# A second set of buffers for the front of a pair, the residual added on TensorE, and small products split into two row halves

## What is computed

```
block 0   attention in 8x8 windows, 4 heads of 12 channels, with a bias table; x = x + proj(attn)
          g = a * sigmoid(b), (a, b) = w1 x;  x = x + leaky(conv3x3(pad_edge(g)))
block 1   x  = x + dwconv3x3_cpe1(x)
          y  = layernorm over channels (x);  act = silu(W_act y);  y = W_in y
          t  = silu(dwconv3x3(y));  q, k = elu(W_qk t) + 1;  v = t
          z  = 1 / (q . mean(k));  kv = rope(k)^T v per head;  attn = (rope(q) kv) z + dwconv3x3_lepe(v)
          x  = x + W_out(attn * act)
          x  = x + dwconv3x3_cpe2(x)
          x  = x + W_fc2 gelu(W_fc1 layernorm(x))
```

## Time and profile before

| | |
|---|---|
| median of 3 runs | 790.66 us (789.95 to 791.23) |
| the profiled execution | 786.9 us |
| its span on the core | 784.9 us |
| PE busy | 671.9 us (86%), mean granted clock 0.898 |
| DVE busy | 528.8 us (67%) |
| ACT, POOL busy | 423.4 us, 312.9 us |

### The profile page before, as it was taken

One profiled execution on the slowest core, in us unless ns is written; L12 is line 12 of the kernel. 1 busy time (PEld: TensorE's weight loads), 2 busy tenths in 40 slices (PEclk: granted clock), 3 DMA queues, 4 the chain that ended last, 5 costly groups with the idle time before them and its releaser, 6 DMA issues. The chain is left out here.

```text
span 784.9 us, 21749 instructions
## 1 busy us (share of the span) xinstructions
PE 671.9 (86%) x9580; PEld 385.9 (49%) x9580; DVE 528.8 (67%) x575; ACT 423.4 (54%) x517; POOL 312.9 (40%) x200
## 2 busy tenths in 40 slices
PE   5899989879899999876888999888987994686795
PEld 3576545547545555445644455465433442562242
DVE  6668307999989434599889333899992128998702
ACT  3578237958464386585342587685304755513334
POOL 8433301547655211115965120138870000677300
PEclk9999999979989999897979999977899996555799
DMA  4200122000001022100000122000000110000001
GB/s 101 56 21 18 44 67 63 18 2 18 4 15 32 18 63 56 38 17 2 18 1 2 32 63 63 17 2 2 2 1 15 50 50 26 1 3 0 1 2 46
DMA packets 19471, 20.55 MB, mean 26 GB/s; under 512 B 8784, under 2 KB 18128, under 8 KB 19378
## 3 DMA queue, kind: packets, MB, share of 16 engines
q1 hardware_dynamic: 17810, 18.95, 8.9%
q10 hardware_dynamic: 1568, 0.22, 0.2%
HBM read 8.39 MB, written 3.54 MB: 15 GB/s over the span
## 5 line engine op out<-in xcount | busy, mean ns | idle before, releaser
L1400 POOL TENSOR_TENSOR SC<-SC,mx 128x768 f32<-128x768 f32 x48 | 81.8, 1705 | 218.5 <-DVE mx L1200 218.5
L1258 DVE SCALAR_TENSOR_TENSOR CT<-TP,vec_sb,CT 112x768 f32<-112x768 f32 x96 | 148.5, 1566 | 0.8
L658 PE MATMUL ps<-ZP,wdw 48*64 48x384 f32 x1728 | 145.9, 488 | 3.4 <-DMA ZP<-YF 2.4
L1244 DVE SCALAR_TENSOR_TENSOR QS<-ZP,vec_sb,QS 112x768 f32<-112x768 f32 x96 | 111.9, 1200 | 0.6
L658 PEld LDWEIGHTS ps<-ZP,wdw 48*64 48x64 f32 x1728 | 73.3, 134 | 73.5 <-issue 34.2
L1196 DVE TENSOR_TENSOR SC<-ps,bias_sb 128x768 f32<-128x768 f32 x48 | 45.7, 952 | 63.0 <-PE ps L723 35.5
L658 PE MATMUL ps<-G,w_sb 48*64 48x384 f32 x864 | 75.1, 499 | 1.7 <-DVE X1T L1213 1.4
L1230 DVE TENSOR_TENSOR LV<-LV,XB 112x768 f32<-112x768 f32 x24 | 25.5, 1064 | 73.1 <-ACT LV L1048 73.1
L942 ACT ACT_TABLE_LOAD x52 | 66.7, 1283 | 0.9
L1371 POOL TENSOR_TENSOR KC<-KK,rope_th_sb 98x384 f32<-98x384 f32 x12 | 18.0, 1496 | 106.2 <-DVE KK L1264 106.1
L658 PEld LDWEIGHTS ps<-G,w_sb 48*64 48x64 f32 x864 | 36.4, 138 | 39.1 <-issue 30.6
(11 more groups left out here) (166 smaller groups left out, 1239.4 us busy)
## 6 DMA issues: line engine op xcount, KB each, us to landing
ZP<-YF SPq DMA_DIRECT2D x48, 75.0 KB, 2.2
XR<-in_x_dram SPq DMA_DIRECT2D x24, 144.0 KB, 2.8
X1T<-in_x_dram SPq DMA_DIRECT2D x24, 144.0 KB, 2.8
XA<-XB SPq DMA_DIRECT2D x48, 72.0 KB, 2.2
out_dram<-XB SPq DMA_DIRECT2D x24, 144.0 KB, 2.3
rope_th_sb<-in_rope_th_dram SPq DMA_DIRECT2D x1, 441.0 KB
w_sb<-in_w_dram SPq DMA_DIRECT2D x2, 81.0 KB, 2.6
wfc_sb<-in_wfc_dram SPq DMA_DIRECT2D x4, 36.0 KB
```

The lines of the kernel that those rows point to most:

```text
L658: mm = pe.matmul(slot(job)[half(c, HALF), r * BANK:r * BANK + SPX], w[half(r), tap * HALF:(tap + 1) * HALF], shifted(t, d * CROWS + c * WI ...
L1244: dve.scalar_tensor_tensor(out=rows16(T0[n]), in0=win, scalar=wt, in1=rows16(T0[n]), op0=ALU.mult, op1=ALU.add).then_inc(dwc_step, 1)
L1258: dve.scalar_tensor_tensor(out=ct, in0=win, scalar=wt, in1=ct, op0=ALU.mult, op1=ALU.add).then_inc(lepe_step, 1)
L1400: pool.tensor_tensor(sc, sc, bc_last(mx[:, (q % NSC) * 12:(q % NSC) * 12 + 12], TOK), ALU.subtract).then_inc(sub_ready, 1)
```

## The change

What it does:
- ZP is kept for block 0's result and d0 alone. A second padded image ZI takes what ie and oz write, and c1 and d3 read it. py of pair i+1 waits for d0 of pair i in place of d3; ie of pair i+1 waits for d3 of pair i.
- x3 writes XF, a state buffer of its own, freed by op; xc and yn read it. The layer norm of the front works in two buffers LF, that of the back and z in the two chunks left of LV.
- XA and pa are gone. op now multiplies in two column halves and adds the state by products of XF with an identity (eye2) into the same PSUM sums: 4 + 4 matmuls in place of 2. oz adds only a bias.
- tr, kt and vt are done in two row halves: 12, 16 and 16 products in place of 6, 8 and 8, each with half the contraction rows and half the columns streamed; the halves write different PSUM banks, and pt, ke, ko, kr, ve and kv read the new layout.
- For space: PT has 5 buffers in place of 6, KC and KS one in place of two (so kr waits for the kv before), kv_turn shares km_sb.
- All five order strings are new.

Of the order strings only the stretch around the last front stands here; the rest of the diff is cut to what carries it.

```diff
@@ PE_ORDER
-    q.2.0@3 av.3.2@0 kv.2.0@2 kt.2.1@1 pj.3.2@0 q.2.1@2 w1a.3.1@1 kt.2.2@0 q.2.2@3 vt.2.1@1 vt.2.2@0 kv.2.1@1
-    w1b.3.2@1 kv.2.2@0 kp.2.0@0 w1a.3.2@2 dn.2.2@0 dn.2.0@3 cv.3.0@1 at.2.0@3 dn.2.1@2 cv.3.1@1 at.2.1@0 op.2.0@1
-    cv.3.2@2 op.2.1@0 at.2.2@1 d3.2.0@0 xc2.2.0@0 va2.2.0@0 op.2.2@1 f11.2.0@0 d3.2.1@1 f10.2.0@0 xc2.2.1@1 f12.2.0@3
-    va2.2.1@1 d3.2.2@0 f2.2.0@3 xc2.2.2@0 f10.2.1@1 f12.2.1@2 va2.2.2@0 f11.2.1@3 d0.3.0@1 f2.2.1@0 f11.2.2@2
-    f10.2.2@3 xc.3.0@1 d0.3.1@0 f12.2.2@3 va.3.0@2 xc.3.1@0 f2.2.2@3 va.3.1@0 d0.3.2@1 ip.3.0@0 ip.3.1@2 ac.3.0@3
+    cv.3.1@0 kv.2.2@2 q.2.1@3 kp.2.0@2 q.2.2@0 dn.2.0@2 cv.3.2@1 dn.2.1@3 at.2.0@2 dn.2.2@0 d0.3.0@1 op.2.0@2 at.2.1@3
+    xc.3.0@2 d0.3.1@1 op.2.1@3 d0.3.2@2 xc.3.1@1 at.2.2@0 d3.2.0@1 op.2.2@0 va.3.1@1 va.3.0@3 d3.2.1@0 ip.3.0@1
+    ip.3.1@3 d3.2.2@2 xc2.2.1@1 ac.3.0@0 xc2.2.0@3 xc.3.2@1 va2.2.0@3 va.3.2@1 va2.2.1@3 f11.2.0@1 ip.3.2@3 f10.2.0@0
...
@@ DVE_ORDER
+    az.2.1 am.2.1 c20.2.2 c21.2.2 c22.2.2 c23.2.2 c24.2.2 c25.2.2 c26.2.2 c27.2.2 oz.2.1 az.2.2 c28.2.2 am.2.2 oz.2.2
+    yn.3.0 yn.3.1 c10.3.0 c11.3.0 c12.3.0 c13.3.0 c14.3.0 yn2.2.0 c15.3.0 yn.3.2 c16.3.0 yn2.2.1 c17.3.0 c10.3.1
...
@@ SP: py
-                        wait_filled(sp, last(*[("d3", i - 1, d) for _, d in near(i, n)]))
+                        wait_filled(sp, last(*[("d0", i - 1, d) for _, d in near(i, n)]))
...
-                elif name == "pa":
-                    wait_read(sp, ("d0", i, n))
-                    if i:
-                        wait_read(sp, ("op", i - 1, n))
...
@@ PE: tr, kt, op
-                    for j in range(6):
-                        mm = pe.transpose(slot(job)[:, j * 128:(j + 1) * 128], SC[q % NSC][:, j * 128:(j + 1) * 128],
-                                          ident_sb[:, :])
+                        for r in range(2):
+                            at = r * BANK + j * HALF
+                            mm = pe.transpose(slot(job)[:, at:at + HALF],
+                                              SC[q % NSC][half(r, HALF), j * 128:(j + 1) * 128],
+                                              ident_sb[half(r, HALF), half(r, HALF)])
...
-                        mm = pe.matmul(slot(job)[0:TT, j * 128:j * 128 + R],
-                                       two_rows(1 + n * CROWS + 2 * j, K1), wlk_sb[:, :], start=True, stop=True)
+                        for r in range(2):
+                            rows = slice(r * HALF, r * HALF + C + 1)
+                            mm = pe.matmul(slot(job)[0:TT, r * BANK + j * C:r * BANK + (j + 1) * C],
+                                           two_rows(1 + n * CROWS + 2 * j, rows), wlk_sb[rows, 0:C],
+                                           start=True, stop=True)
...
-                    product(job, wq("out"), CT[(i * CH + n) % 2])
+                    wait_slot(pe, job)
+                    image = [half(c, HALF if c == 0 else C) for c in range(2)]
+                    for b in range(2):
+                        for c in range(2):
+                            pe.matmul(slot(job)[image[c], b * BANK:b * BANK + SPX], wq("out")[:, image[c]],
+                                      CT[(i * CH + n) % 2][:, b * SPX:(b + 1) * SPX], start=True, stop=False)
+                    for r in range(2):
+                        for c in range(2):
+                            at = n * CPX + c * SPX
+                            mm = pe.matmul(slot(job)[image[c], r * BANK:r * BANK + SPX],
+                                           eye2_sb[half(r), 0:HALF if c == 0 else C],
+                                           XF[half(r), at:at + SPX], start=False, stop=True)
...
@@ ACT: x3, ie
-                        act.wait_ge(stored[n], 32 * i)
-                    act.activation(pairs(chunk(XB, n)), two(job), ACT.Identity, bias=v("cpe1_b"))\
+                        wait_filled(act, ("op", i - 1, n))
+                    act.activation(pairs(chunk(XF, n)), two(job), ACT.Identity, bias=v("cpe1_b"))\
...
-                    wait_filled(act, ("d0", i, halo_last(n)))
-                    act.activation(inner8(ZP, n), two8(job), ACT.Identity, bias=inp_b2).then_inc(free(job), 2)
+                    if i:
+                        wait_filled(act, last(*[("d3", i - 1, d) for _, d in near(i, n)]))
...
+                    act.activation(inner8(ZI, n), two8(job), ACT.Identity, bias=inp_b2).then_inc(free(job), 2)
...
@@ DVE: oz
-                    dve.wait_ge(xa_placed[n], 64 * (i + 1))
-                    dve.scalar_tensor_tensor(out=inner8(ZP, n), in0=two8(job), scalar=v("out_b"),
-                                             in1=chunk(XA, n).rearrange("p (b y x) -> p b y x", b=2, x=W),
-                                             op0=ALU.add, op1=ALU.add).then_inc(free(job), 2)
+                    dve.tensor_scalar(inner8(ZI, n), two8(job), v("out_b"), None, ALU.add).then_inc(free(job), 2)
...
@@ POOL: kr
+                old = before(i, n, 1)
+                if old:
+                    wait_filled(pool, ("kv",) + old)
```

More of the change, by code:

```diff
@@ L46 @@
 SQ = ["q", "k", "v", "w1a", "w1b", "act", "inp", "lq", "lk", "out"]
-KEPT = ["act", "inp", "out"]
+KEPT = ["out"]
 TURN = ["q", "k", "w1a", "w1b"]
@@ L894, in run @@
                     pe.wait_ge(yn2_ready, YN2_COUNT["yn2", i, n])
-                    turned(job, wfc1_sb[:, m * HALF:(m + 1) * HALF], chunk(LV, n))
+                    turned(job, wfc1_sb[:, m * HALF:(m + 1) * HALF], nbuf(n))
                 elif name == "f2":
@@ L1041, in run @@
                     wait_filled(act, job)
-                    act.activation(pairs(chunk(LV, n)), two(job), ACT.Square).then_inc(free(job), 2)
+                    old = before(i, n, NFR)
+                    if name == "sq" and old:
+                        wait_filled(act, last(("ip",) + old, ("ac",) + old))
+                    if name == "sq2" and n >= NFR:
+                        wait_filled(act, last(*[(f"f1{m}", i, n - NFR) for m in range(FG)]))
+                    dst = LF[kc % NFR] if name == "sq" else nbuf(n)
+                    act.activation(pairs(dst), two(job), ACT.Square).then_inc(free(job), 2)
                 elif name in ("rs", "rs2"):
@@ L1045, in run @@
                     wait_filled(act, job)
-                    act.activation(pairs(chunk(LV, n)), two(job), ACT.Ln, bias=eps_ln).then_inc(free(job), 2)
+                    dst = LF[kc % NFR] if name == "rs" else nbuf(n)
+                    act.activation(pairs(dst), two(job), ACT.Ln, bias=eps_ln).then_inc(free(job), 2)
                     wait_read(act, job)
-                    act.activation(chunk(LV, n), chunk(LV, n), ACT.Exp, scale=-0.5)\
+                    act.activation(dst, dst, ACT.Exp, scale=-0.5)\
                        .then_inc(rstd_ready if name == "rs" else rstd2_ready, 1)
@@ L1070, in run @@
                     wait_filled(act, job)
-                    act.activation(KK[n % 2].rearrange("p (t c) -> p t c", c=R),
-                                   slot(job)[0:TT, :].rearrange("p (t c) -> p t c", c=128)[:, :, 0:R],
-                                   ACT.Exp, bias=minus1[0:TT, :]).then_inc(free(job), 1)
+                    act.activation(pairs(KK[n % 2]), two(job, TT), ACT.Exp, bias=minus1[0:TT, :])                       .then_inc(free(job), 1)
                 elif name == "qe":
@@ L1085, in run @@
                         wait_filled(act, ("kv",) + old)
-                    act.activation(VT.rearrange("p (t b c) -> p t b c", b=2, c=C),
-                                   slot(job)[0:TT, :].rearrange("p (t b c) -> p t b c", b=2, c=HALF)[:, :, :, 0:C],
-                                   ACT.Copy).then_inc(free(job), 2)
+                    act.activation(pairs(VT), two(job, TT), ACT.Copy).then_inc(free(job), 2)
                 elif name == "z":
@@ L1091, in run @@
                     wait_filled(act, job)
-                    act.activation(pairs(chunk(LV, n)), two(job), ACT.Ln, bias=eps_z).then_inc(free(job), 2)
+                    if n >= NFR:
+                        act.wait_ge(am_ready, AM_COUNT["am", i, n - NFR])
+                    act.activation(pairs(zbuf(n)), two(job), ACT.Ln, bias=eps_z).then_inc(free(job), 2)
                     wait_read(act, job)
-                    act.activation(chunk(LV, n), chunk(LV, n), ACT.Exp, scale=-1.0).then_inc(z_ready, 1)
+                    act.activation(zbuf(n), zbuf(n), ACT.Exp, scale=-1.0).then_inc(z_ready, 1)
                 elif name[:2] == "ge":
@@ L1314, in run @@
                     wait_filled(dve, job)
-                    dve.tensor_tensor(pairs(chunk(LV, n)), two(job), pairs(chunk(LV, n)), ALU.mult).then_inc(free(job), 2)
+                    dve.tensor_tensor(pairs(zbuf(n)), two(job), pairs(zbuf(n)), ALU.mult).then_inc(free(job), 2)
                 elif name == "am":
```

306 lines of the change are left out of this document (154 added, 152 removed).

## The result

The changed kernel takes 715.59 us (median of 4 runs, 712.72 to 719.18) beside 790.83 us (4 runs) for the kernel before: a ratio of 0.906, 95% interval 0.9025 to 0.9091, 75 us less. The profiled execution took 712.72 us, its span is 710.9 us. Ratios are taken from fast runs alone, and only e6 has slower ones: 723.28 and 722.01 of its four, which leaves 711.05 and 719.76.

What follows compares the result with a forecast made beforehand. PE and DVE waiting for each other in turn was taken as the bound. Start 125.3 + W 454 + last gap 2 + end 141.7 = 723.0, + 5.8 to the median = 728.8 us; range 700 to 770.

Steps and rivals of the forecast that it cites:

- W: Stretch from pair 0's first tap to pair 2's last d3: 489.2 us before, 454 forecast with PE at 88%.
- The last gap: Between pair 2's last d3 and pair 3's first tap: 2 us in place of 34.9, which gives 32.9.
- The other two gaps: From last d3 of pairs 0 and 1 to the next first tap, 47.4 and 36.8 us: merge with the tap stretches.
- W's work: PE's full-rate work in W: 417.0 after moves, +4 for op, -21.5 for the halves, in sum 399.5 us.
- op: Output projection with the residual added by identity products: 1.49 to 1.93 us each, +4 us over nine in W.
- The end: From pair 3's first tap to the kernel's end: 141.7 us, 6.2 more for pair 2's back on DVE.
- The start: From the kernel's begin to pair 0's first tap: kept at 125.3 us.
- W doesn't shrink: Rival, 16%: PE stays at 82% as DVE's taps and the chain to d3 set W at 487; 762 us.
- Loads pass one by one: Rival, 10%: loads of the row halves in tr, kt and vt run serially; W 498, 773 us.
- the slower case: Rival, 8%: neither loads nor streams of the halves overlap, tr takes 2.2 us; W 574, 849 us.
- PE at 95%: Rival, 8%: PE reaches 95% of full rate in the middle; W 420, 695 us.
- It doesn't do what it says: Rival, 6%: ie behind d3, and ts, hold pair 3's first tap as long as now; 785 to 795 us.

Runs made afterwards that it cites:

- e6: Changed kernel with the ninth tap of the first depthwise convolution done for one row in sixteen only: 720.88 us, ratio 0.908.
- e4: Changed kernel with only pair 3's front put back behind the last d3 of pair 2 on PE and ACT's list following: 746.46 us, ratio 0.9455.
- e1: Changed kernel with the transpositions tr in one piece again, all else kept: 717.09 us, ratio 0.9088.
- e7: Changed kernel with tr, kt and vt all in one piece, buffers, orders and identity products kept: 716.05 us, ratio 0.9093.
- e10: Changed kernel without the output projection's identity products and with the ninth tap for one row in sixteen only: 716.10 us, ratio 0.9095.
- e8: Changed kernel with the twelve evictions oz moved from DVE to ACT, nothing left out: 771.6 us, ratio 0.9783.
- e5: Changed kernel without the identity products of the output projection, so the state is not added: 715.25 us, ratio 0.9089.
- e12: Changed kernel with 23 groups of idle products in PE's waits of the last pair, written to PSUM slots already free: 712.55 us, ratio 0.9009.
- e3: Kernel before with nothing changed but tr in two row halves and its eviction: 785.67 us, ratio 0.9937.
- e2: Changed kernel with the output projection's identity products ahead of the wait for ym, same work: 715.67 us, ratio 0.905.

## Why the prediction was right, and where it was not

I forecast a span of 723.0 us and 728.8 us by the median; it is 710.9 and 715.6. The difference of 12.1 in the span is +8.1 (start), -25.0 (W to the last d3), -0.4 (the last gap) and +5.2 (end), so the parts were off by more than the sum. That the total is off by 12 us and not by 25 is luck: the start and the end cost 13 us for which I had added nothing.

- **The last gap**, 34.9 to 2 us: 1.6. Exact, and e4 shows it as a price in latency: putting the front back costs 30.9 us and brings a gap of 29.9. The step held with its mechanism (one eviction behind d3 and the start of the tap).
- **The other two gaps.** By the same means they went from 47.4 and 36.8 to 3.3 and 3.5. I booked them only through "W's work over its efficiency". That is the step that failed in its form: W did not become work divided by a share. PE works in W at 396.1/429.0 = 92% (151.15 x 0.99 + 3.30 + 128.04 x 0.99 + 3.50 + 117.57 x 0.96 = 396), where I took 88% with an upper end of 95%. 399.5/0.88 was 454, 25 us more than came. And the 92% is no limit of PE: with tr whole (e1), with all halves whole (e7, 9 us more PE work in W), with 21 us less in one stretch (e4), W does not follow by more than the 5 us in which two profiles of one kernel differ. DVE, 83% busy in it, doesn't set it either (e10). What is left is the chain of hand-overs, am, ym, op, oz, d3, ie: e8 delayed one of its links and W grew by 51 us. That the link counts is shown; that this chain and nothing else makes the 429 us is argued.
- **W's work**, 399.5: 396.1. The sum is near and its terms are not, which is luck too. The gains of kt and vt were put far too high and tr's for one job too low, which the next rows show, and some 12 us of work that I left in W went into the start.

Single jobs in PE's timelines, first of the changed kernel (one tr and two in a row, vt, kt at the upper clock, kt at the lower), then of the kernel before (kt and vt at the upper clock):

```profile
293.96 0.59 PE L734 MATMUL ps<-ident_sb,SC 64*128 64x64 f32 x12
229.71 0.96 PE L734 MATMUL ps<-ident_sb,SC 64*128 64x64 f32 x24 [1.49 <-DVE X1T L1239]
590.09 0.59 PE L831 MATMUL ps<-ident_sb,TP 48*98 48x48 f32 x16
594.90 1.59 PE L812 MATMUL ps<-wlk_sb,TP 49*98 49x48 f32 x32 [0.69 <-ACT TP L1096]
580.03 2.90 PE L812 MATMUL ps<-wlk_sb,TP 49*98 49x48 f32 x32 [1.42 <-ACT LV L1067]
...
148.70 1.62 PE L811 MATMUL ps<-wlk_sb,TP 113*98 113x96 f32 x16
194.79 0.97 PE L828 MATMUL ps<-ident_sb,TP 112*98 112x112 f32 x8
```

kt takes 1.59 us in halves and 1.62 whole, at the upper clock both times: a gain of 0.03, not 0.97. The 2.92 that I took from the chain was a job at the lower clock, and so were vt's 1.66 and the 2.64 of the sums kv from which I priced the halves (granted clock 0.50 at all three); W's sum takes them as work at the full rate. Nor does the price hold at one level: kt in halves takes 2.90 at the lower clock, where I had 1.95. For vt, 0.97 to 0.59 is -0.38, where I had 1.66 to 0.98. tr was under-estimated: another twelve add 0.96 - 0.59 = 0.37 us, where another six whole ones added 0.61 (1.48 for twelve, 0.87 for six), -0.24 for a job and not -0.14.

Also, I booked all 48 tr in W, and only 26 lie there (32 before the change). In W that makes 26 x 0.24 + 9 x 0.03 + 9 x 0.38 = 9.9 in place of 21.5, near the 9 us that e7 puts back. The other 22 lie in the start, whose work grew by 6.5 us all the same, so 6.5 + 22 x 0.24 = 11.8 us moved into it. With op's real size (below, 9 x 0.64) my sum would be 417.0 + 5.8 - 9.9 - 11.8 = 401; the 5 us to the 396 measured stay open.

The rule that I had set against the halves (the Trainium skill, TensorE: Matmul & The Clock Gate, section LDWEIGHTS: a load takes the time of its columns whatever its rows) holds for one load, at the shortest 157 ns for 49 rows of 98 columns where the earlier trace rows had 161 for 113; but the loads overlap, 32 of them (at least 5.0 us in sum) within kt's 1.59 us, so nothing got slower. The section Packing small matmuls — row/col tiling of that page says that loads pass beside running products only in other rows of the array. The trace doesn't bear out the "only": in the kernel before, 16 loads over all the rows (at least 2.6 us in sum) lie within kt's 1.62 us. Yet the term as a whole was worth nothing that the total shows (e7).
- **op**, 1.49 to 1.93: 2.1 at the upper clock, and twice that in the end. The changed kernel's products with w_out and with the identity, at the upper and at the lower clock:

```profile
517.47 1.50 PE L898 MATMUL ps<-CT,wsq_sb 112*64 112x384 f32 x8 [1.31 <-POOL CT L1443]
518.91 0.87 PE L903 MATMUL ps<-XF,eye_sb 48*64 48x384 f32 x8
...
641.98 2.82 PE L898 MATMUL ps<-CT,wsq_sb 112*64 112x384 f32 x8
644.73 1.51 PE L903 MATMUL ps<-XF,eye_sb 48*64 48x384 f32 x8
```

From start to start and with the next job, the second four add 0.69 us (518.91 to 519.60) and the first 1.44: 2.13, 0.20 more than I had. In the last pair the first op takes 4.3 us. In W its weight is not settled (e5); in the end it is waited for.
- **The end**, 141.7: 146.9, 11.4 above the 135.5 of before. DVE has the six instructions of pair 2's back there, as I put it (6.2 us), but its work in the end rose only from 92.2 to 93.5 us: the taps took less (1132 ns for 1196 among c1, 1464 for 1552 among c2; why is not known). What grew is DVE's idle time, from 43.3 to 53.4 us, for which I had added nothing in the end. The longest new wait in it is the one ahead of c20.3.2, in the changed kernel and then in e5:

```profile
646.40 1.43 DVE L1283 TENSOR_SCALAR CT<-TP,vec_sb 112x768 f32<-112x768 f32 x1 [4.20 <-PE ps L903]
...
646.22 1.01 DVE L1277 TENSOR_SCALAR CT<-TP,vec_sb 112x768 f32<-112x768 f32 x1 [2.72 <-PE ps L898]
```

c20.3.2 writes the buffer that op.3.0 reads, and op.3.0 stands behind at.3.1 and dn.3.2 in PE's list and runs at the lower level, 4.3 us in place of 2.9; the kernel before has no such wait. The earlier trace rows had shown a clock of 0.59 among the last taps, and I took nothing from it for products on the path. Without the identity products the wait is 1.5 us shorter (e5), which d3.3.0 took back; under the higher clock of e12 it is under 1 us, and the end 3 to 4 us shorter. The rest of the 10 us is spread over shorter waits and stays open.
- **The start**, 125.3 as before: 133.4. DVE has 80.6 us of work in it where it had 65.6, PE 117.3 for 110.8: the new order does more of pair 1's block 0 ahead of the first tap. It is moved work, not lost: the first pair-to-pair distance is 160.5 in place of 197.4. I had held the start fixed, and should have counted the jobs that stand ahead of c10.0.0 in the new lists.
- **Rivals.** "W doesn't shrink" fell (430.6 beside 524.1, by the measure with the gap). "Loads pass one by one" and the slower case fell on tr's 0.37 and kt's 1.59. "PE at 95%", 695 us, was the nearest in W (420, and 429 came) and wrong in start and end. "It doesn't do what it says" fell on the 1.6 us.
- **Small terms.** kr, oz and PT: nothing to be seen of them at a size that matters; DVE's oz takes 1.01 us as before. None was tried by itself.

What each part gives, as far as runs show it: the buffers with the new orders nearly all of the 75 us (e7 against before: 0.9093), the last gap alone 31 of it (e4), while the other two gaps were not put back by themselves; the halves 0 to 2 us (e1, e7), 5 in the old kernel for tr alone (e3); the identity products cost nothing that the total shows (e5, e2). The buffers without the new orders were not tried.
